# Routed mixture of experts: weight columns as the stationary operand of the wide product, with the expert's columns copied to a ring

## The reference

```python
logits = xt @ w_gate
top_logits, sel = jax.lax.top_k(logits, TOP_K)          # TOP_K = 2 of E = 8
probs = jax.nn.softmax(top_logits, axis=-1)
h = silu(einsum('td,edh->eth', xt, w1)) * einsum('td,edh->eth', xt, w3)   # D = 128, H = 256
y = einsum('eth,ehd->etd', h, w2)
out = einsum('ktd,tk->td', y[sel.T, t], probs)
```

## Time and profile before

| | us |
|---|---|
| median of 3 executions | 2713.99 |
| lowest, highest | 2692.0, 2717.08 |
| the profiled execution | 2702.98 |
| its span, first to last instruction | 2701.2 |
| mean granted PE clock in it | 0.88 |
| first tile loop, from its first to its last wide product | 1602.3 to 1818.8 |
| second tile loop | 2434.0 to 2662.8 |

### The profile page before, as it was taken

The page is one execution under the profiler, slowest core; times in us unless marked ns, Lnnn a source line. Parts: engine busy times, 40 slices in busy tenths (PEclk is TensorE's granted clock), DMA queues, the critical chain, the costliest instruction groups (busy, mean ns, idle before and its releaser), DMA issues. The chain is left out here.

```text
span 2701.2 us, 41099 instructions
## 1 busy us (share of the span) xinstructions
PE 2223.7 (82%) x11854; PEld 1331.9 (49%) x11854; DVE 1669.5 (62%) x4556; ACT 1290.8 (48%) x2278; POOL 1369.9 (51%) x1337
## 2 busy tenths in 40 slices
PE   5477998998799899999999748578999999847673
PEld 3344655666656566644444435344444444334442
DVE  8866775775677577666666534236877787453232
ACT  6642553333445433256666314344667777423331
POOL 7524653442275434266666561327857666164322
PEclk8696998998979899989999859788999999757786
DMA  1001112221011122200000222220000000032232
GB/s 48 2 0 41 37 25 80 88 84 45 9 46 45 28 96 95 100 17 1 1 1 1 62 65 75 70 72 21 17 3 1 1 0 1 1 101 68 78 93 58
DMA packets 113864, 113.22 MB, mean 42 GB/s; under 512 B 22776, under 2 KB 93560, under 8 KB 113400
## 3 DMA queue, kind: packets, MB, share of 16 engines
q1 hardware_dynamic: 105464, 93.92, 11.7%
q0 software_dynamic: 8192, 16.79, 2.1%
HBM read 72.50 MB, written 25.43 MB: 36 GB/s over the span
## 5 line engine op out<-in xcount | busy, mean ns | idle before, releaser
L2393 DVE TENSOR_REDUCE l_diffneg_max<-psum 128x1 fp32r<-128x512 f32 x512 | 336.3, 685 | 94.1 <-PE psum L2131 89.8
L2308 ACT ACTIVATE l_diffweights<-psum 128x1024 f32<-128x1024 f32 x256 | 262.0, 1026 | 144.7 <-PE psum L2160 142.8
L2131 PE MATMUL psum<-l_diffkz,l_diffQ 128*128 128x512 f32 (+1 forms) x512 | 241.0, 489 | 8.0 <-DVE l_diffneg_max L2393 6.9
L2945 ACT ACTIVATE l_lightswapped<-psum 32x512 f32<-32x512 f32 x304 | 179.0, 589 | 100.9 <-DVE l_lightturned L3037 97.5
L4857 PE MATMUL psum<-l_moe1w,l_moe1gt 128*128 x680 | 116.8, 298 | 133.3 <-ACT l_moe1gt L4943 55.1
L4857 PEld LDWEIGHTS psum<-l_moe1w,l_moe1gt 128*128 128x128 f32 x680 | 102.4, 206 | 240.1 <-issue 240.1
L5106 DVE COPY open_y<-psum 128x128 f32<-128x128 f32 x170 | 49.5, 291 | 274.5 <-PE psum L4857 162.4
L1657 DVE TENSOR_REDUCE l_attn0neg_max<-psum 128x1 fp32r<-128x512 f32 x256 | 167.3, 683 | 51.5 <-PE psum L1388 48.8
L4841 PE MATMUL psum<-l_moe1w,l_moe1zt 128*128 x340 | 191.6, 648 | 0.0
L1563 ACT ACTIVATE l_attn0weights<-psum 128x1024 f32<-128x1024 f32 x128 | 130.4, 1023 | 117.0 <-PE psum L1410 116.9
L5219 POOL DMA_INDIRECT l_moe1yb<-results,open_back_idx x80 | 76.6, 957 | 207.6 <-DMA results<-open_y 184.5
(11 more groups left out here) (607 smaller groups left out, 6137.5 us busy)
## 6 DMA issues: line engine op xcount, KB each, us to landing
l_moe0bcs<-gate_rows SPq DMA_DIRECT2D x64, 512.0 KB
l_moe1xt<-sorted SPq DMA_DIRECT2D x170, 64.0 KB
results<-open_y SPq DMA_DIRECT2D x82, 128.0 KB
l_attn0Q<-l_attn0q_hi SPq DMA_DIRECT2D x128, 64.0 KB
l_moe1w<-in_moe_w SPq DMA_DIRECT2D x6, 1024.0 KB
l_attn0Q<-l_attn0q_lo SPq DMA_DIRECT2D x64, 64.0 KB
sorted<-l_moe1spare SPq DMA_DIRECT2D x54, 64.0 KB, 1.5
l_moe0w_raw<-in_moe_w SPq DMA_DIRECT2D x20, 128.0 KB, 5.2
```

Of the source, the lines that this page charges most:

```text
L2131: nc.tensor.matmul(ps[:, bank, :], Q[rows, n % 4, st * P:(st + 1) * P], kz[rows, n % 4, hh, :], start=True, stop=True).then_inc(pe_max.sem ...
L2308: nc.scalar.activation(weights[:, tt, 2 * pair:2 * pair + 2, :], ps[:, S[m % 2]:S[m % 2] + 2, :], ACT.Exp, scale=SCALE).then_inc(act_exp.s ...
L2393: nc.vector.tensor_reduce(neg_max[:, n % 2, st, row:row + 1], ps[:, bank_of(("max", n, b)), :], AXX, ALU.max, negate=True).then_inc(vec_ma ...
L2945: copy = lambda to, frm: nc.scalar.activation(to, frm, ACT.Copy)
```

## The change

The wide product is turned round. The expert's weight columns become the stationary operand and the tile's 128 tokens the moving one: four matmuls of 128 columns in place of one of 512. The result then has hidden units on partitions and tokens along the columns, so that g is already the stationary operand that `down` needs. The transposes of g, their copy, their tile `gt`, their PSUM bank and their semaphores go.

The stationary operand is no longer read at an offset out of `w`. A ring `here` of 4 slots of 512 columns is added. DVE copies a tile's 256 columns of w1 into it (`w1_here`) and ACT its 256 columns of w3 (`w3_here`), both at a register's offset. Three copies of each are made ahead of the loop; inside, round n makes those of tile n+3. A copy waits for `up` of the tile four before it. On ACT it stands last in the round, after tile_turned(n+2); on DVE it stands right after product_g(n).

Register loads are made for up to eight tiles of a chunk at a time (`experts_from`), by PE, DVE and ACT each for itself, without the check of the bounds. PE needs the value for `down` alone. The wait for the loaded weights moves from `up` to the two copies and `down`. The slot of g is free once `down` of two tiles before has ended, not the transposes.

```diff
+    HERE_RING = 4
+    AT_ONCE, CLAMPED = 8, "the table's rows and columns are clamped by minima where they are made"
...
-        rows = sb("rows", [P, NSEQ, NQ, P])
+        rows, here = sb("rows", [P, NSEQ, NQ, P]), sb("here", [P, HERE_RING, 4 * P])
...
-        s, g, gt, y = sb("s", [P, 2, 2 * P]), sb("g", [P, 2, 2 * P]), sb("gt", [P, 2, 2 * P]), core.late_rows.y
+        s, g, y = sb("s", [P, 2, 2 * P]), sb("g", [P, 2, 2 * P]), core.late_rows.y
...
+        def experts_from(engine, n):
+
+            c = max(c for c in range(R.CHUNKS) if R.FIRST_TILE[c] <= n)
+            at, many = n - R.FIRST_TILE[c], min(AT_ONCE, R.FIRST_TILE[c] + R.TILES[c] - n)
+            _, found = nc.values_load_multi_w_load_instructions(table[0:1, c, W_AT + at:W_AT + at + many], engines=[engine.engine], min_val=0,
+                                                                max_val=7 * R.COLS, skip_runtime_bounds_check_because=CLAMPED)
+            return {n + k: value for k, value in enumerate(found)}
...
-            def up(n, w_at):
+            def up(n):
                 pe_up.start()
+                wait(t, vec_here, n, "w1")
+                wait(t, act_here, n, "w3")
+                wait(t, act_zt, n, "zt")
+                wait(t, vec_g, n - 2, "g")
+                for k in range(4):
+                    ins = nc.tensor.matmul(ps[:, H[n % 2], k * P:(k + 1) * P], here[:, n % HERE_RING, k * P:(k + 1) * P], zt[:, n % 2, :], start=True, stop=True)
+                ins.then_inc(pe_up.sem, pe_up.step("up"))
+
+            def down(n, w_at):
+                pe_down.start()
                 if n == 0:
                     t.wait_ge(w_loaded, 48)
-                wait(t, act_zt, n, "zt")
-                wait(t, vec_g, n - 2, "g")
-                nc.tensor.matmul(ps[:, H[n % 2], :], zt[:, n % 2, :], w[:, bass.ds(w_at, 4 * P)], start=True, stop=True
-                                 ).then_inc(pe_up.sem, pe_up.step("up"))
-
-            def g_turned(n):
-                pe_gt.start()
-                wait(t, act_gt, n - 1, "gt")
                 wait(t, vec_g, n, "g")
-                for h in range(2):
-                    ins = nc.tensor.transpose(ps[:, GT, h * P:(h + 1) * P], g[:, n % 2, h * P:(h + 1) * P], core.ident[:, :])
-                ins.then_inc(pe_gt.sem, pe_gt.step("gt"))
-
-            def down(n, w_at):
-                pe_down.start()
-                wait(t, act_gt, n, "gt")
                 wait(t, vec_y, n - 1, "y")
                 for h in range(2):
-                    ins = nc.tensor.matmul(ps[:, Y, 0:P], gt[:, n % 2, h * P:(h + 1) * P], w[:, bass.ds(w_at + (4 + h) * P, P)],
+                    ins = nc.tensor.matmul(ps[:, Y, 0:P], g[:, n % 2, h * P:(h + 1) * P], w[:, bass.ds(w_at + (4 + h) * P, P)],
                                            start=h == 0, stop=h == 1)
                 ins.then_inc(pe_down.sem, pe_down.step("down"))
...
-                    at_w[0] = expert_of(0)
+                    at_w.update(experts_from(t, 0))
                     tile_turned(0)
                     tile_turned(1)
-                up(n, at_w[n])
+                up(n)
                 if n + 1 < R.ALL:
                     if n + 1 in R.FIRST_TILE:
                         wait(t, vec_table, R.FIRST_TILE.index(n + 1), "row")
-                    at_w[n + 1] = expert_of(n + 1)
+                    if n + 1 not in at_w:
+                        at_w.update(experts_from(t, n + 1))
                 if n >= 2:
                     down(n - 2, at_w.pop(n - 2))
                 if n + 2 < R.ALL:
                     tile_turned(n + 2)
-                if n >= 1:
-                    g_turned(n - 1)
                 if n == R.RANKED:
                     ranks(NSEQ - 1)
                 if opening and n == R.ALL - 2:
                     opening.turned(t, TOK)
             down(R.ALL - 2, at_w[R.ALL - 2])
-            g_turned(R.ALL - 1)
             down(R.ALL - 1, at_w[R.ALL - 1])
...
-                act_gt.start()
-                wait(a, pe_gt, n, "gt")
-                wait(a, pe_down, n - 2, "down")
-                act(gt[:, n % 2, :], ps[:, GT, 0:2 * P], ACT.Copy).then_inc(act_gt.sem, act_gt.step("gt"))
-
+            def w3_here(n):
+                act_here.start()
+                if n == 0:
+                    a.wait_ge(w_loaded, 48)
+                if n in R.FIRST_TILE:
+                    wait(a, vec_table, R.FIRST_TILE.index(n), "row")
+                if n not in at_w:
+                    at_w.update(experts_from(a, n))
+                wait(a, pe_up, n - HERE_RING, "up")
+                act(here[:, n % HERE_RING, 2 * P:4 * P], w[:, bass.ds(at_w.pop(n) + 2 * P, 2 * P)], ACT.Copy).then_inc(act_here.sem, act_here.step("w3"))
+
+            at_w = {}
...
+            w3_here(0)
+            w3_here(1)
             tile_turned(0)
             tile_turned(1)
+            w3_here(2)
             for n in range(R.ALL):
                 silu(n)
                 if n + 2 < R.ALL:
                     tile_turned(n + 2)
-                if n >= 1:
-                    g_turned(n - 1)
+                if n + 3 < R.ALL:
+                    w3_here(n + 3)
...
+            def w1_here(n):
+                vec_here.start()
+                if n == 0:
+                    d.wait_ge(w_loaded, 48)
+                if n in R.FIRST_TILE:
+                    wait(d, vec_table, R.FIRST_TILE.index(n), "row")
+                if n not in at_w:
+                    at_w.update(experts_from(d, n))
+                wait(d, pe_up, n - HERE_RING, "up")
+                v.tensor_copy(here[:, n % HERE_RING, 0:2 * P], w[:, bass.ds(at_w.pop(n), 2 * P)]).then_inc(vec_here.sem, vec_here.step("w1"))
+
+            at_w = {}
+
             def product_g(n):
                 vec_g.start()
                 wait(d, act_silu, n, "silu")
-                wait(d, pe_gt, n - 2, "gt")
+                wait(d, pe_down, n - 2, "down")
...
+            for n in range(3):
+                w1_here(n)
             for n in range(R.ALL):
                 if n >= 2:
                     result(n - 2)
                 product_g(n)
+                if n + 3 < R.ALL:
+                    w1_here(n + 3)
```

More of the change, by code:

```diff
@@ L4645, in routed_block @@
     nc, plan, ps, R = core.nc, core.plan, core.psum, Routed
-    ZT, H, GT, Y, TOK, LOGITS, RANKS = 0, (1, 2), 3, 4, 5, 6, 7
+    ZT, H, Y, TOK, LOGITS, RANKS = 0, (1, 2), 4, 5, 6, 7
     SLOTS, PAIR_SLOTS = 10, 4
     ROW_AT, W_AT, PAD_AT = 0, 64, 128
+    HERE_RING = 4
+    AT_ONCE, CLAMPED = 8, "the table's rows and columns are clamped by minima where they are made"
     chunk_of = lambda j: max(c for c in range(R.CHUNKS) if R.FIRST[c] <= j)
@@ L4794, in _ @@
         def _(t):
-            for of in (pe_tr, chooser.pe_gate, pe_rank, pe_zt, pe_up, pe_gt, pe_down):
+            for of in (pe_tr, chooser.pe_gate, pe_rank, pe_zt, pe_up, pe_down):
                 of.credit(t)
@@ L4822, in ranks @@
                 ins.then_inc(pe_rank.sem, pe_rank.step("rank"))
-            def expert_of(n):
-                c = max(c for c in range(R.CHUNKS) if R.FIRST_TILE[c] <= n)
-                at = W_AT + n - R.FIRST_TILE[c]
-                return t.value_load(table[0:1, c, at:at + 1], min_val=0, max_val=7 * R.COLS)
             def tile_turned(n):
@@ L4908, in _ @@
         def _(a):
-            for of in (act_z, act_hi, act_zt, act_silu, act_gt):
+            for of in (act_z, act_hi, act_zt, act_silu, act_here):
                 of.credit(a)
@@ L4961, in _ @@
                     opening.weights_high(a)
-            g_turned(R.ALL - 1)
         @block.vector
         def _(d):
-            for of in (vec_stats, vec_shift, vec_lo, chooser.vec_gate, vec_table, vec_place, vec_back, vec_weight, vec_g, vec_y, vec_add):
+            for of in (vec_stats, vec_shift, vec_lo, chooser.vec_gate, vec_table, vec_place, vec_back, vec_weight, vec_g, vec_y, vec_add, vec_here):
                 of.credit(d)
```

4 lines of the change are left out of this document (2 added, 2 removed).

## The result

The changed kernel took 2720.8 us (median of 20 runs, 2700.2 to 2730.4), the kernel before 2706.7 beside it: ratio 1.0039, interval 1.0022 to 1.0057. It is slower by 0.4%, some 10 us by the ratio and 14 by the medians. I had forecast 0.6% faster: the time lies inside the range, the direction was wrong.

A forecast was written before the change was run, and what follows sets the result against it. PE's instruction stream was taken to bound the dense tiles. Terms of -25.3, +4.5 (DVE) and +5 (start) gave -16 us, so 2698 us off the median (chance 0.50), with a range of 2672 to 2736.

The forecast's parts named there:

- the dense period: Undisturbed tiles of both loops: PE's stream falls by 0.19 us a tile, from 1.63 to 1.44 us.
- Rivals 3, 4 and 5: Rival 4: eight register values load one after another, 33 us more, 2731 us, chance 0.05; rival 3 and rival 5 below.
- rival 5: Wide product: weight loads don't hide behind products, 1.5 us a tile, 200 us in sum, 2914 us; chance 0.02.
- The 133 tiles: Dense tiles counted in both loops, of 170; at 0.19 us each they give a ceiling of 25.3 us.
- the start: Start of each loop: register load and copy delay the first wide product; 2.5 us per loop, 5 us in sum.
- the bursts: Gather bursts: their end is set by POOL's 24 untouched indirect DMA issues, so no change was taken.
- rival 2: Bursts: DVE copies and POOL's indirect DMAs exclude each other, 47 us more, 2745 us; chance 0.16.
- Rival 1: Gather bursts: fewer handovers let two more tiles through each, 11.5 us more gain, 2686 us; chance 0.14.
- Where DVE sets the pace: Weighted sums and table work on DVE: PE waits one copy longer after each, 4.5 us; ends 0 and three times that.
- 66.5 dense tiles: Dense tiles of the first loop, of 85: their 125 us hold 108 us of PE stream and 17 of stalls.
- SP: nothing added: SP's register load and issues stay one set per tile; priced at nothing, other end 0.2 us a tile.
- rival 3: Dense period stays 1.63 us, held by DVE, ACT or SP handovers; only the start costs, 2719 us; chance 0.13.

The follow-up runs named there:

- runs 12 and 15: 12: changed kernel with two result banks, split sums and spread padding, ratio 0.9913; 15: the same with all copies on ScalarE, 0.9901.
- run 13: The kernel before with split sums and padding transfers spread behind tiles 14 to 21; ratio 0.9955, loops 441.2 us.
- run 2: The changed kernel without copies after tile 3 or the register loads feeding them, leaving work out; ratio 1.0014, loops 446.1 us.
- run 8: The changed kernel with two PSUM banks in turn for the results, on the second chip; ratio 0.9969 to the kernel before.
- run 5: The kernel before with each sequence's weighted sum split in two pieces, on the second chip; ratio 0.9961.

## Why the prediction was wrong

**Right: the dense period.** -0.19 forecast, 1.63 to 1.45 measured. 1.45 is 13 records of 0.11 us. Rivals 3, 4 and 5 fall with it (rival 5's 2914 should have been 2898, since it left out the forecast's -16). The 133 tiles would have given 24 us, and in runs 12 and 15, where little holds the loop, most of the gain is there: 18 and 22 us of loops under run 13. On weight loads, the eight records with eight loads of 0.19 us each take 0.89: they hide. The part of the Trainium skill that I cited for rival 5 ("TensorE: Matmul & The Clock Gate", Part 3) is not borne out for these full 128-row products.

**Right in kind, somewhat more in size: the start.** VectorE ended placing at 1598.7 and the first wide product began at 1599.86, 1.2 us later; tiles 0 to 5 took 2.2 us more in each loop. Together that is 3.4 us for the 2.5 forecast, inside its range of 0.8 to 4.2; to tile 14 it is 2.2 to 4.3 us on top of the 1.2.
```profile
1598.53 0.15 DVE L5048 TENSOR_TENSOR l_moe1run<-l_moe1base,psum 128x8 f32<-128x8 f32 x1
1599.51 0.70 DVE L5111 COPY l_moe1here<-l_moe1w 128x256 f32 x3 [0.82 <-issue]
```
```profile
1599.86 2.08 PE L4848 MATMUL psum<-l_moe1zt,l_moe1here 128*128 128x128 f32 x8 [1.01 <-DVE l_moe1here L5111]
```

**Right: the bursts.** POOL's operations kept 0.95 us and 0.30 between them, so that rival 2 falls, and with it, for this shape, the rule on ports of the Trainium skill ("SBUF — State Buffer", "Who interferes with whom") as a cost. In the changed kernel's trace 28 of the 170 copies ran beside one of POOL's operations, and they took 0.29 us like the others. Rival 1's gain isn't there either: tiles 40 to 44 took 36.9 and 36.6 us for 36.1 and 36.6.
```profile
1694.68 0.97 POOL L5243 DMA_INDIRECT l_moe1yb<-results,open_back_idx  x1 [0.30 <-issue]
1695.96 0.95 POOL L5243 DMA_INDIRECT l_moe1yb<-results,open_back_idx  x1 [0.30 <-issue]
```

**Failed, first step: "Where DVE sets the pace".** I charged one copy behind each of eight holds, 4.5 us, at most three times that. Two things were left out. First, what a hold costs is its length less the time for which PE still has work. Before, VectorE was away from 1733.38 to 1737.76, 4.38 us, and PE ran on for 2.25 (to 1735.63). After, VectorE was away from 1736.37 to 1740.95, 4.58 us, the copy being the 0.20 more, and PE ran on for only 1.9 (to 1738.27), since a shorter stream is used up sooner. The wait grew by 0.55 us where I had 0.28. Where a register load falls into the round of a sum, as at tile 52, it is on top: 0.51 us of wait before, 1.84 after, 0.88 without load and copy (run 2). Second, and larger: the clock fell behind such waits. I read the granted clock of 0.99 as a property of the stretch, not as something that a change could take away. At the sum of tile 45 the rounds come to 6.3 us over the period against 2.9, so 3.4 more where I had 0.28. My 66.5 dense tiles had 17 us of stalls beside their stream, and I didn't ask what stood in them. Splitting the sums gave back 16 us of both loops.

**Failed, second step: "SP: nothing added ... I price it at nothing".** I looked at the per-tile work only. At the border SyncE spends 8 us on padding ahead of the stores and of the next chunk's first load. Before, 1.63 us tiles nearly reached over that (tiles 26 to 40: 23.6 and 23.3, against 22.8 of stream); at 1.45 they don't (24.6 and 23.7, against 20.3). Spreading it gave 14.6 us on top of two banks and split sums, 5 to 8 alone. My other end was 0.2 us on every tile, 27 us in sum. It was wide enough, but as a longer period (rival 3), which is not what came.

The forecast's -16 and the measured +10 are 26 us apart, and 22 to 23 of them are missing in the dense stretches of the loops. Of these, 11 are more waiting there (7.9 to 19.2 us), and the rest is work at the lower clock and waits too short to be listed. The repairs, the second bank among them, give the changed kernel 29 to 32 us and before 4 to 7, a difference of 22 to 28. So these two steps account for most of the miss; the start and the stretch between the loops have a few us in it.

**What stays open:** what the second bank is worth alone on the first kind of chip; what decides behind which wait the clock falls; by which of its two ways the padding acts; why the first five tiles cost 2 us more even without the later copies (25.6 us in run 2); and the stretch between the loops, with the stop at L2160.

## What to carry to other kernels

When a change shortens the period of a pipelined loop, list every hold that a period used to cover (long work of a helper engine, a run of issues on a DMA queue), and charge each with the run-ahead that is lost, not only with what is added to it. Look at the granted clock behind the present holds: here a wait that grew from 2.64 to 3.19 us was followed by two tiles at half clock. If the gain doesn't arrive, cut the holds before giving up the change: here the changed kernel was 0.4% slower than before with them, and 0.9 to 1.0% faster once they were cut, of which the same cuts, without the second bank, gave the kernel before 0.45%. The look at the clock doesn't tell in advance which wait it will fall behind.

## What was not expected of the hardware

One register load of eight values took 556 to 767 ns in the median, where one of a single value took 302: a load has a large fixed part, and eight at once are far from eight loads.

On the second chip before took 2527 us instead of 2710. There the bursts of indirect DMAs at the gathers didn't slow PE at all. POOL's operations are as long as elsewhere, 0.95 us and 0.30 apart, but tiles 40 to 44 took 5.8 us instead of 36.5 and 70 to 75 took 7.3 instead of 26 to 38. A window over such a burst in run 8, columns as in the earlier trace rows, in which PE is busy 86% of the time at 0.97; in the changed kernel's 1690 to 1726 it was 11.40 of 36 us at 0.68:
```profile
1658.00:1710.00 52.00, 44.88 (x381) 44.02 (x380) 33.14 (x123) 28.14 (x88) 24.86 (x27) 0.97 0.42 114
```
So the burst's 1.4 us steps are not in the indirect DMAs as such. In the version of before on that chip (run 5) tiles 40 to 44 took 6.5 us. No run here shows what makes the difference between the chips.
